# Two graph layers on one core: attention scores as additions of spread keys instead of a TensorE product, and the plain fp32 neighbour sum

## The chip, the cores and the metric

One core of a Trainium2 chip. The metric is the device time of one execution in microseconds (us). A core has five engines, each working through its own queue in order: TensorE (PE; its weight loads are shown as PEld), VectorE (DVE), ScalarE (ACT), GpSimd (POOL) and SyncE (SP, which issues transfers). They meet only through semaphores.

## The reference

128 graphs of 128 nodes, 256 features each, go through two layers; everything is fp32.

```
h  = relu(layernorm(x));  x = x + adj @ (h @ w0) + b0
h  = relu(layernorm(x))
proj = h @ fc_w + fc_b                      # 8 heads of 256
q, k = proj @ q_w + q_b, proj @ k_w + k_b   # one number per node and head
s  = leaky_relu(q + k^T + (1 - adj) * -1e9)
out = softmax(s) @ proj                     # per head
x  = x + sigmoid(concat_heads(out) @ fp_w + fp_b + h)
```

A score is the sum of one number of the row's node (the query) and one of the column's node (the key), plus a mask.

## The kernel before, in words

The graphs go in 64 pairs (`J` = 2). Per pair p, layer 0 first sums the neighbours (`aggregate`, lines 317 to 329), then multiplies with w0 (`transform`, 331), adds x and the bias (`residual0`, 537), takes the statistics (`stats1`, `mean1`) and turns the normalised tile (`transpose_h`, 339). Layer 1 works on heads whose fc and fp weights were multiplied together once in the setup (`fold`, lines 259 to 272): `project(p, q, n)`, n = 0 to 7, writes two heads of one graph into one PSUM bank; `attend(p, j, c)` multiplies them with the transposed attention rows of graph j and head group c (four heads), accumulating in `ybank`.

Precision comes from splitting: a matrix is stored as a high part rounded to fp32r and the rest (`_hi`, `_lo`), and `split` (246 to 251) sums three fp32r products of the parts. ACT writes the high part from PSUM (`g_high`, `pT_high`, `hT_high`), DVE the low part (`g_low`, `pT_low`, `hT_low`).

The scores are a TensorE product. `queries_keys` (349) makes 64 rows of keys and queries; DVE splits them (`kq_high`, `kq_parts`) and multiplies the keys with a mask of heads into `rk`, 32 partitions by 1024 (`spread`, 571); ACT writes the queries into the stationary tile `lq` (`queries`, 753). `scores(p, q, j, c)` (366) is one matmul with 512 columns into the only bank `sbank`; it waits until DVE has read the bank's last tenant. DVE adds the mask and takes the minimum (signs are turned) in `mask_min` (594), once per head, then `leaky` (605, a scalar_tensor_tensor of `att` with itself), ACT `exp` with row sums, DVE `inverse`, POOL `normalise` (918), PE `transpose_p`.

`aggregate` before: ACT writes the high part of h0 and of adjT (`h0_high`, `aT_high`), POOL the low parts (`h0_low`, `aT_low`), four times a 256-column and a 128-column fp32r matmul give two sums, ACT copies the small one (`ah_small`), DVE forms a difference (`ah_rest`) and POOL adds them (`ah_low`).

PSUM has eight banks: two for `front` (sums, kq, out0, h1T), `ybank`, `sbank`, and four `gbank`, which a ring of twelve tenants per pair shares, eight of `project` and four of `transpose_p` (`RING`, line 29; `ring_free`, 303).

Each engine's order within a pair is written out by hand in its `step(i, q)`. `pipeline` (172) runs steps before and after a hardware loop whose body holds two steps. PE at step i works on pair i, on the end of pair i - 1 and on layer 0 of pair i + 1. SP per pair loads `g_in` (x, adj, adjT: 512 KB) and stores `res` (256 KB). The setup begins with ten plain fp32 matmuls on ones (`warm`, 253), whose result nothing reads; the profile shows each plain fp32 matmul as two records.

```
def scores(p, q, j, c):
    bank = scores_free(NC * j + c, p)
    pe.matmul(bank[:], lq[q][j][:], rk[q][:, c * HC:(c + 1) * HC, :], start=True, stop=True)
```

Of the kernel before, what the change touches and what calls it, by code (L numbers as in the profile page):

```python
# [10 lines left out]
P = 128  # L11
D = 256
DT = D // P
H = 8
# [9 lines left out]
ROWS = 64  # L24
KEYS = 32
# [5 lines left out]
SRING = ((0, 0), (1, 0), (2, 0), (3, 0))  # L31
G_RANK = (0, 1, 0, 1, 0, 1, 1, 0)


def gnn_pair(nc, graph, identity, head_mask, row_coef, w0, bias0, fc_wT, fc_b, qk_w, q_b, k_b, fp_w, fp_b, out):
# [6 lines left out]
    with ExitStack() as ctx:  # L42
# [9 lines left out]
        def two(name, shape, dt=F32):  # L52
            return [sb(f"{name}{k}", shape, dt) for k in range(2)]

        def sems(name, n):
# [4 lines left out]
        hmask = sb("hmask", [P, H, P])  # L60
        coef = sb("coef", [P, 10])
# [4 lines left out]
        u_none = sb("u_none", [P, J, DT, ROWS])  # L66
# [3 lines left out]
        kqb2 = sb("kqb2", [P, 2])  # L70
# [6 lines left out]
        gate = sb("gate", [P, 8])  # L77
# [3 lines left out]
        early = sb("early", [P, 4, J * D])  # L81
        h0_f, xb = [[early[:, 2 * n + k, :].rearrange("p (j d) -> p j d", j=J) for k in range(2)] for n in range(2)]
        h0_hi, h0_lo = two("h0_hi", [P, J, D], F32R), two("h0_lo", [P, J, D], F32R)
        aT = two("aT", [P, J, 2, P], F32R)
        aT_lo, aT_hi = [[t[:, :, k, :] for t in aT] for k in range(2)]
        t_pos = two("t_pos", [P, J, P])
        ah_s, ah_d = sb("ah_s", [P, J, DT, P]), sb("ah_d", [P, J, DT, P])
        ah_hi, ah_lo = two("ah_hi", [P, J, DT, P], F32R), two("ah_lo", [P, J, DT, P], F32R)
        late = sb("late", [P, 8, J * D])
        x1, h1, feats_c, res = [[late[:, 2 * n + k, :].rearrange("p (j d) -> p j d", j=J) for k in range(2)]  # L90
                                for n in range(4)]
# [8 lines left out]
        kq_h, kq_t = sb("kq_h", [ROWS, P], F32R), sb("kq_t", [ROWS, P], F32R)  # L100
        lq = [two(f"lq{k}", [P, P], F32R) for k in range(2)]
        rk = two("rk", [P, H, P], F32R)
# [10 lines left out]
        fcT_sb = [w.rearrange("p (t d) -> p t d", d=D)  # L113
                  for w in (att_all[:, 0:H * D], late[:, 4:8, :].rearrange("p a b -> p (a b)"))]
# [3 lines left out]
        front = psum("front", [P, 2 * BANK])  # L118
        ybank = psum("ybank", [P, BANK])
        sbank = [psum("sbank", [P, BANK])]  # L120
        gbank = [psum(f"gbank{k}", [P, BANK]) for k in range(4)]
        sums = front[:].rearrange("p (j t c n) -> p j t c n", j=J, t=DT, c=2)
        kq = front[:, 0:BANK]
        out0 = kq.rearrange("p (j d) -> p j d", j=J)
        h1T = front[:, BANK:2 * BANK].rearrange("p (j t n) -> p j t n", j=J, t=DT)
# [3 lines left out]
        s_loaded, s_stored = sems("s_loaded", 2), sems("s_stored", 2)  # L129
# [4 lines left out]
        a_none, a_w0hi, v_w0lo, a_uhi, v_ulo, a_rk, v_lq = [  # L134
            sem(n) for n in ("a_none", "a_w0hi", "v_w0lo", "a_uhi", "v_ulo", "a_rk", "v_lq")]

        v_st0, v_mv0, g_ve0, g_rs0, g_nm0, g_nmr0 = [sem(n) for n in ("v_st0", "v_mv0", "g_ve0", "g_rs0", "g_nm0", "g_nmr0")]
        a_h0f, a_h0hi, g_h0lo, a_aThi, g_aTlo = [sem(n) for n in ("a_h0f", "a_h0hi", "g_h0lo", "a_aThi", "g_aTlo")]
        g_xb, g_t = sem("g_xb"), sem("g_t")
        pe_ah, a_ahhi, a_ahs, v_ah = [sem(n) for n in ("pe_ah", "a_ahhi", "a_ahs", "v_ah")]  # L140
        g_ahlo, pe_out0, v_x1 = [sem(n) for n in ("g_ahlo", "pe_out0", "v_x1")]
        v_st1, v_mv1, g_ve1, g_rs1, g_nm1, g_nmr1 = [sem(n) for n in ("v_st1", "v_mv1", "g_ve1", "g_rs1", "g_nm1", "g_nmr1")]
        a_h1, g_feats, pe_zT, a_hThi, v_hTlo = [sem(n) for n in ("a_h1", "g_feats", "pe_zT", "a_hThi", "v_hTlo")]
        pe_kq, v_kqh, v_kqt, v_rk, a_lq = [sem(n) for n in ("pe_kq", "v_kqh", "v_kqt", "v_rk", "a_lq")]
        pe_g, a_g, v_g = sems("pe_g", J * GC), sems("a_g", J * GC), sems("v_g", J * NC)
        pe_s, v_mx, v_leaky = sems("pe_s", J * NC), sems("v_mx", J * NC), sems("v_leaky", J * NC)
# [18 lines left out]
        def rows_of(u, j, dt):  # L165
            return u[:, j, dt, :].rearrange("p (k g c h) -> p k g c h", k=2, g=J, c=2)[:, :, j, :, :]

        def u_of(m, dt):
            return m[:, dt, :, D:D + 2].rearrange("p h k -> p k h").unsqueeze(2).bitcast(F32)\
                .broadcast_to([P, 2, 2, H])  # L170

        def pipeline(eng, step, behind, ahead):

            first = behind + 2
            last = first + (NP - ahead - first) // 2 * 2
            for i in range(-ahead, first):
                step(i, i % 2)
            with eng.Fori(first, last, 2) as i:
                step(i, first % 2)
                step(i + 1, 1 - first % 2)  # L180
            for i in range(last, NP + behind):
                step(i, i % 2)
# [15 lines left out]
        def _(sp):  # L198
# [5 lines left out]
            def setup():  # L204
                load(0, 0)
                weights(0)
                sp.dma_start(qk[:], qk_w).then_inc(s_small, 16)
                sp.dma_start(fcb[:], fc_b).then_inc(s_small, 16)
# [5 lines left out]
                sp.dma_start(coef[:], row_coef).then_inc(s_rest, 16)  # L214
                sp.dma_start(kqb2[:, 0:1], k_b.partition_broadcast(P)).then_inc(s_rest, 16)
                sp.dma_start(kqb2[:, 1:2], q_b.partition_broadcast(P)).then_inc(s_rest, 16)
# [12 lines left out]
            def store(p, q):  # L229
                sp.wait_ge(g_res, p + 1)  # L230
                sp.dma_start(out[p].rearrange("n (j d) -> n j d", j=J), res[q]).then_inc(s_stored[q], 16)
# [798 lines left out]
```

## Time and profile before

| | |
|---|---|
| time of the runs, median (3 runs, 1526.04 to 1527.67 us) | 1526.6 us |
| the profiled execution: its own time, its span | 1527.26 us, 1525.4 us |
| PE busy | 1510.1 us (99%) |
| PEld, DVE, ACT, POOL busy | 1339.6, 1343.5, 1205.1, 933.4 us (88%, 88%, 79%, 61%) |
| mean of the transfers | 37 GB/s, 55.89 MB |
| mean granted TensorE clock | 0.997 |

The span runs from the first to the last instruction. Busy time is the union of an engine's instructions, and these overlap: a matmul's record is longer than the distance to the next one, so costs on PE are read from starts, not from durations. An instruction's duration includes time in which it was held up.

### The profile page before, as it was taken

The numbers are of one execution on the slowest core, as the hardware profiler recorded it, in microseconds if no ns is written. First come the engines' busy times: TensorE is split into PE (matmuls) and PEld (weight loads), VectorE is DVE, ScalarE is ACT, GpSimd is POOL, SyncE is SP. The second block draws the span as 40 slices with busy tenths as digits, with TensorE's granted clock in tenths as the row PEclk, the third lists the DMA queues.
The fourth block names the chain that finished last, engine by engine and source line by source line (L and its number), as shares of the span: only waits on it lengthen the run. The fifth ranks groups of instructions, "written<-read, shape, count | busy, mean of one in ns | idle before, by whom it ended". The sixth has DMA issues, their size and how long they took to land.

```text
span 1525.4 us, 32795 instructions
## 1 busy us (share of the span) xinstructions
PE 1510.1 (99%) x9816; PEld 1339.6 (88%) x9816; DVE 1343.5 (88%) x4720; ACT 1205.1 (79%) x3674; POOL 933.4 (61%) x1226
## 2 busy tenths in 40 slices
PE   7999999999999999999999999999999999999998
PEld 6888888888888888888888888888888888888887
DVE  6988988988988989889889889889898898898886
ACT  5887878878878778878788787788788787887875
POOL 3656666566566566666665665665666666656653
PEclk9999999999999999999999999999999999999999
DMA  5101101101001011011011010010110110110100
GB/s 182 36 22 42 41 21 41 41 21 41 30 32 41 21 41 41 21 41 41 21 41 41 21 41 29 33 41 21 41 41 21 41 41 21 41 41 21 41 14 15
DMA packets 22579, 55.89 MB, mean 37 GB/s; under 512 B 2976, under 2 KB 5408, under 8 KB 22560
## 3 DMA queue, kind: packets, MB, share of 16 engines
q1 hardware_dynamic: 22560, 55.67, 10.6%
q8 instruction: 8, 0.13, 0.0%
q14 instruction: 11, 0.09, 0.0%
HBM read 38.88 MB, written 16.78 MB: 36 GB/s over the span
## 4 chain that ended last, share of the span: by engine, by line
PE 97%; DVE 1%; issue 1%; DMA 0%; ACT 0%; POOL 0%; SPq 0%; POOLq 0%; DVEq 0%
PE gbank L250 47%; PE ybank L250 23%; PE front L250 9%; PE gbank L375 7%; PE sbank L368 4%; PE front L327 3%; PE front L343 2%; PE gbank L270 1%; PE front L328 1%; DMA fcb<-fc_b_dram 0%; DVE att L601 0%; DVE att L608 0%; DVE g_lo L581 0%; DVE rk L573 0%; POOL att L921 0%
## 5 line engine op out<-in xcount | busy, mean ns | idle before, releaser
L921 POOL TENSOR_TENSOR att<-att,rinv 128x512 f32<-128x512 f32 x256 | 266.4, 1041 | 348.8 <-DVE rinv L613 348.8
L769 ACT ACTIVATE att<-att 128x128 f32<-128x128 f32 x1024 | 397.3, 393 | 65.8 <-DVE att L608 65.7
L250 PE MATMUL gbank<-m_hi,hT_lo 128*128 128x512 f32 x1024 | 417.4, 408 | 0.4 <-DVE g_lo L581 0.4
L250 PE MATMUL gbank<-m_lo,hT_hi 128*128 128x512 f32 x1024 | 405.2, 396 | 0.0
L250 PE MATMUL gbank<-m_hi,hT_hi 128*128 128x512 f32 x1024 | 404.1, 395 | 0.0
L762 ACT ACTIVATE g_hi<-gbank 128x512 fp32r<-128x512 f32 x512 | 286.8, 585 | 97.4 <-PE gbank L250 97.3
L581 DVE TENSOR_TENSOR g_lo<-gbank,g_hi 128x512 fp32r<-128x512 f32 x512 | 348.3, 680 | 15.4 <-ACT g_hi L762 15.4
L250 PE MATMUL ybank<-g_hi,pT_lo 128*128 128x256 f32 x1024 | 299.8, 293 | 0.0
L250 PE MATMUL ybank<-g_hi,pT_hi 128*128 128x256 f32 x1024 | 289.7, 283 | 0.0
L250 PE MATMUL ybank<-g_lo,pT_hi 128*128 128x256 f32 x1024 | 289.6, 283 | 0.0
L601 DVE CUSTOM_DVE_ANT_0 att<-sbank,t_pos 128x128 f32<-128x128 f32 x1024 | 236.3, 287 | 14.4 <-issue 14.4
L250 PEld LDWEIGHTS gbank<-m_hi,hT_hi 128*128 128x128 f32 x1024 | 194.6, 190 | 47.4
L608 DVE SCALAR_TENSOR_TENSOR att<-att 128x516 f32<-128x516 f32 x256 | 232.3, 927 | 0.0
L250 PEld LDWEIGHTS gbank<-m_hi,hT_lo 128*128 128x128 f32 x1024 | 194.3, 190 | 31.5 <-DVE g_lo L581 0.8
L250 PEld LDWEIGHTS gbank<-m_lo,hT_hi 128*128 128x128 f32 x1024 | 194.6, 190 | 29.7
L250 PEld LDWEIGHTS ybank<-g_lo,pT_hi 128*128 128x128 f32 x1024 | 195.9, 191 | 5.4
L250 PEld LDWEIGHTS ybank<-g_hi,pT_lo 128*128 128x128 f32 x1024 | 195.9, 191 | 0.2 <-DVE pT_lo L588 0.2
L769 ACT ACTIVATION_READ_ACCUMULATOR att<-att 128x1 f32 x1024 | 196.0, 191 | 0.0
L250 PEld LDWEIGHTS ybank<-g_hi,pT_hi 128*128 128x128 f32 x1024 | 195.8, 191 | 0.0
L588 DVE TENSOR_TENSOR pT_lo<-gbank,pT_hi 128x512 fp32r<-128x512 f32 x256 | 171.8, 671 | 1.0 <-ACT pT_hi L776 1.0
L898 POOL TENSOR_TENSOR h_lo<-early,h_hi 128x512 fp32r<-128x512 f32 x64 | 83.0, 1297 | 139.0 <-ACT h_hi L727 138.9
L375 PE MATMUL gbank<-ident,att 128*128 128x128 f32 x1024 | 153.4, 272 | 0.0
(101 smaller groups left out, 3042.3 us busy)
## 6 DMA issues: line engine op xcount, KB each, us to landing
g_in<-graph_dram SPq DMA_DIRECT2D x64, 512.0 KB, 3.3
out_dram<-late SPq DMA_DIRECT2D x64, 256.0 KB, 2.0
fp_sb<-fp_w_dram SPq DMA_DIRECT2D x4, 512.0 KB, 8.2
att<-fc_wT_dram SPq DMA_DIRECT2D x2, 512.0 KB, 6.4
late<-fc_wT_dram SPq DMA_DIRECT2D x2, 512.0 KB, 8.0
hmask<-head_mask_dram SPq DMA_DIRECT2D x1, 512.0 KB, 8.7
w_f<-w_dram SPq DMA_DIRECT2D x1, 256.0 KB, 7.2
b_row<-bias_dram SPq DMA_DIRECT2D x1, 128.0 KB, 6.9
```

What stands on the lines that cost most here:

```text
L250: mm = pe.matmul(out_ap, w, m, start=first and n == 0, stop=last and n == len(terms) - 1)
L327: pe.matmul(sums[:, j, dt, :, :], h0_hi[q][:, j, s], aT[q][:, j, :, :], start=True, stop=False)
L368: pe.matmul(bank[:], lq[q][j][:], rk[q][:, c * HC:(c + 1) * HC, :], start=True, stop=True)\
L375: mm = pe.transpose(bank[:, h * P:(h + 1) * P], att[j][c][:, h * P:(h + 1) * P], ident[:])
L581: dve.tensor_tensor(g_lo[j][:, s], bank[:], g_hi[j][:, s].bitcast(F32), ALU.subtract)\
L588: dve.tensor_tensor(pT_lo[j][:, hs, :], rows, pT_hi[j][:, hs, :].bitcast(F32), ALU.subtract)\
L601: r = dve.tensor_tensor_reduce(a[:, s], bank[:, s], t_pos[q][:, j, :], 1.0, 3.0e38, ALU.add, ALU.min, a[:, CH + h:CH + h + 1])
L608: dve.scalar_tensor_tensor(out=a, in0=a, scalar=SLOPE, in1=a, op0=ALU.mult, op1=ALU.min)\
L762: act.activation(g_hi[j][:, s], gbank[tenant(RING, 4, ("g", n), p)[0]][:], ACT.Copy).then_inc(a_g[n], 1)
L769: e = act.activation(a[:, s], a[:, s], ACT.Exp, scale=-1.0, bias=a[:, CH + h:CH + h + 1], accum_out=esum[j][c][:, h:h + 1])
L898: gp.tensor_tensor(h0_lo[q][:], h0_f[q], h0_hi[q][:].bitcast(F32), ALU.subtract)\
L921: gp.tensor_tensor(a, a, rinv[j][c][:].unsqueeze(2).broadcast_to([P, HC, P]), ALU.mult)\
```

## The change

- Scores: ACT adds the biases while it copies the key and query rows to SBUF (`kq_rows`). SP writes the 16 key rows to device memory (`keys_out`, 8 KB) and reads them back spread to all 128 partitions (`keys_in`, 8 KB per partition, 1 MB written to SBUF per pair). PE turns the rows once (`turn_queries`, one transpose), so that the queries lie one per partition and head, and ACT copies them (`queries`). POOL adds keys and mask for four heads at a time (`mask_keys`, four per pair, 128x512); DVE adds the query as a per-partition scalar and takes the minimum (`mask_min`, still once per head, now a tensor_scalar with an accumulator output on SBUF). The matmul `scores`, `kq_high`, `kq_parts`, `spread`, `rk`, `lq`, the head mask and its transfer are gone.
- `aggregate`: four plain fp32 matmuls of 128 columns on `h0_f` and adjT as loaded. `h0_high`, `aT_high`, `h0_low`, `aT_low`, `ah_small`, `ah_low` are gone; `ah_rest` now writes the low part itself.
- PSUM: `bank0` (sums, out0), `bank1` (h1T, kq, kqT), `ybank`, `tbank` for all `transpose_p`, and four `gbank` for the eight `project` alone.
- Orders of all engines are new. The loop body holds four steps (`U` = 4), layer 0 runs up to three pairs ahead on PE, `x1` and `feats` have four buffers. `load` runs six pairs ahead and stands in SP's queue before `keys_in`.
- Setup: 18 instead of 10 matmuls on ones; two small loads go to ACT's queue.

```diff
-RING = ((("t", 3), -1), (("g", 2), 0), (("g", 0), 0), (("g", 1), 0), (("g", 4), 0), (("t", 0), 0),
-        (("g", 5), 0), (("g", 3), 0), (("g", 7), 0), (("t", 1), 0), (("g", 6), 0), (("t", 2), 0))
+RING = ((3, 0), (6, 0), (7, 0), (4, 0), (1, 1), (0, 1), (2, 1), (5, 1))
+TRING = ((0, 0), (1, 0), (2, 0), (3, 0))
...
             def load(p, q):
                 if has(p - 2):
                     sp.wait_ge(a_h0f, 2 * (p - 1))
+                    sp.wait_ge(pe_ah, p - 1)
                     sp.wait_ge(g_xb, p - 1)
                     sp.wait_ge(g_t, p - 1)
-                    sp.wait_ge(g_aTlo, p - 1)
...
+            def keys_out(p, q):
+                sp.wait_ge(a_kq, p + 1)
+                sp.dma_start(key_rows[q], kq_sb[q][0:KEYS]).then_inc(s_rows[q], 16)
+            def keys_in(p, q):
+                sp.wait_ge(a_qs, p + 1)
+                sp.wait_ge(s_rows[q], 8 * (p - q % 2) + 16)
+                sp.dma_start(keys[q].rearrange("p j h n -> p (j h n)"),
+                             key_rows[q].rearrange("r n -> (r n)").partition_broadcast(P)).then_inc(s_keys[q], 16)
...
+                if has(i):
+                    store(i, q)
+                if later(i + 6):
+                    load(i + 6, (q + 2) % U)
+                if has(i + 3):
+                    keys_in(i + 3, (q + 3) % U)
+                if has(i + 4):
+                    keys_out(i + 4, q)
...
             def aggregate(p, q):
-                pe.wait_ge(g_h0lo, p + 1)
-                pe.wait_ge(g_aTlo, p + 1)
+                pe.wait_ge(a_h0f, 2 * (p + 1))
                 if has(p - 1):
-                    pe.wait_ge(v_kqt, p)
-                    pe.wait_ge(v_hTlo, p)
-
+                    pe.wait_ge(v_x1, p)
                 for j in range(J):
                     for dt in range(DT):
-                        s = slice(dt * P, (dt + 1) * P)
-                        pe.matmul(sums[:, j, dt, :, :], h0_hi[q][:, j, s], aT[q][:, j, :, :], start=True, stop=False)
-                        mm = pe.matmul(sums[:, j, dt, 1, :], h0_lo[q][:, j, s], aT_hi[q][:, j, :], start=False, stop=True)
+                        mm = pe.matmul(sums[:, j, dt, :], h0_f[q][:, j, dt * P:(dt + 1) * P], adjT_of(q)[:, j, :],
+                                       start=True, stop=True)
...
+            def turn_queries(p, q):
+                pe.wait_ge(a_kq, p + 1)
+                pe.transpose(kqT, kq_sb[q][:], ident[:]).then_inc(pe_kqT, 1)
...
             def transpose_p(p, j, c):
                 pe.wait_ge(g_norm[NC * j + c], p + 1)
-                bank = ring_free(("t", NC * j + c), p)
+                m, pair = tenant(TRING, 1, NC * j + c, p)[1:]
+                if has(pair):
+                    pe.wait_ge(v_pT[m], pair + 1)
...
             def mask_min(p, q, j, c):
-                dve.wait_ge(pe_s[NC * j + c], p + 1)
-                dve.memset(gate[:, 4 + NC * j + c:5 + NC * j + c], 0.0)
+                a = att[j][c]
+                dve.wait_ge(g_keys[NC * j + c], p + 1)
+                dve.wait_ge(a_qs, p + 1)
                 for h in range(HC):
                     s = slice(h * P, (h + 1) * P)
-                    r = dve.tensor_tensor_reduce(a[:, s], bank[:, s], t_pos[q][:, j, :], 1.0, 3.0e38,
-                                                 ALU.add, ALU.min, a[:, CH + h:CH + h + 1])
+                    r = dve.tensor_scalar(a[:, s], a[:, s], qs[q][:, j, c * HC + h:c * HC + h + 1], None, ALU.add,
+                                          ALU.min, accum_out=a[:, CH + h:CH + h + 1])
...
+            def kq_rows(p, q):
+                act.wait_ge(pe_kq, p + 1)
+                if has(p - 2):
+                    act.wait_ge(pe_kqT, p - 1)
+                    act.wait_ge(s_keys[q], 8 * (p - q % 2))
+                act.activation(kq_sb[q][0:ROWS], kq, ACT.Identity, bias=kq_bias[0:ROWS, 0:1]).then_inc(a_kq, 1)
...
+            def mask_keys(p, q, j, c):
+                gp.wait_ge(s_keys[q], 8 * (p - q % 2) + 16)
+                gp.wait_ge(g_t, p + 1)
+                if has(p - 1):
+                    gp.wait_ge(pe_pT[NC * j + c], p)
+                a = att[j][c][:, 0:CH].rearrange("p (h n) -> p h n", h=HC)
+                gp.tensor_tensor(a, keys[q][:, j, c * HC:(c + 1) * HC, :],
+                                 t_pos[q][:, j, :].unsqueeze(1).broadcast_to([P, HC, P]), ALU.add)\
+                  .then_inc(g_keys[NC * j + c], 1)
```

PE's new step, in order: turn_queries(i+1), project(i, 3), attend(i-1, 1, 1), transpose_p(i, 0, 0), project(i, 6), project(i, 7), aggregate(i+3), transpose_p(i, 0, 1), project(i, 4), attend(i, 0, 0), transpose_p(i, 1, 0), project(i+1, 1), transpose_h(i+2), attend(i, 0, 1), project(i+1, 0), queries_keys(i+2), transpose_p(i, 1, 1), attend(i, 1, 0), project(i+1, 2), project(i+1, 5), transform(i+3).

POOL's: mask_keys(i, 1, 0), mask_keys(i, 1, 1), residual1(i-2), normalise(i, 0, 0), inputs(i+2), normalise(i, 0, 1), feats(i), normalise(i, 1, 0), the small ones of variance1(i+2) and variance0(i+4), normalise(i, 1, 1), mask_keys(i+1, 0, 0), mask_keys(i+1, 0, 1).

## Rows read from the trace of the kernel before

**Rows 1.** The page: busy time by engine, and the chain that ended last.
```profile
PE 1510.1 (99%) x9816; PEld 1339.6 (88%) x9816; DVE 1343.5 (88%) x4720; ACT 1205.1 (79%) x3674; POOL 933.4 (61%) x1226
...
PE 97%; DVE 1%; issue 1%; DMA 0%; ACT 0%; POOL 0%; SPq 0%; POOLq 0%; DVEq 0%
```

**Rows 2.** Stretches: us, busy PE, PEld, DVE, ACT, POOL, then clock, DMA share, GB/s.
```profile
0.00:20.00 20.00, 14.67 (x60) 12.62 (x61) 8.87 (x22) 7.99 (x17) 8.08 (x19) 0.83 0.94 312
20.00:40.00 20.00, 16.91 (x93) 13.67 (x91) 18.97 (x68) 12.22 (x30) 8.63 (x13) 1.00 0.14 48
...
700.00:900.00 200.00, 200.00 (x1319) 178.08 (x1318) 177.95 (x630) 159.85 (x484) 124.92 (x164) 1.00 0.09 31
```

**Rows 3.** Timeline of PE, one pair of the loop: start us, us, instruction.
```profile
805.23 0.28 PE L327 MATMUL front<-aT,h_hi 128*128 128x256 f32 x1
...
806.10 0.45 PE L368 MATMUL sbank<-rk,lq 128*128 128x512 f32 x1
806.38 0.28 PE L250 MATMUL ybank<-g_hi,pT_lo 128*128 128x256 f32 x1
...
809.20 0.41 PE L368 MATMUL sbank<-rk,lq 128*128 128x512 f32 x1
809.44 0.60 PE L375 MATMUL gbank<-ident,att 128*128 128x128 f32 x4
809.80 0.48 PE L250 MATMUL gbank<-m_hi,hT_lo 128*128 128x512 f32 x1
...
828.44 0.28 PE L327 MATMUL front<-aT,h_hi 128*128 128x256 f32 x1
```

**Rows 4.** Timeline of PE in the setup, plain fp32, narrow stretches.
```profile
4.70 0.39 PE L257 MATMUL gbank<-ones 128*128 128x128 f32 x2
...
4.92 0.28 PE L257 MATMUL gbank<-ones 128*128 128x128 f32 x1
```

**Rows 5.** Groups of DVE: shapes and count | busy us, mean ns | idle before.
```profile
L601 DVE CUSTOM_DVE_ANT_0 att<-sbank,t_pos 128x128 f32<-128x128 f32 x1024 | 236.3, 287 | 14.4 <-issue 14.4
L608 DVE SCALAR_TENSOR_TENSOR att<-att 128x516 f32<-128x516 f32 x256 | 232.3, 927 | 0.0
...
L573 DVE TENSOR_TENSOR rk<-hmask,kq_t 32x1024 fp32r<-32x1024 f32 x64 | 78.8, 1232 | 2.2
...
L563 DVE TENSOR_SCALAR kq_h<-front,kq_bias,coef 64x128 fp32r<-64x128 f32 x64 | 26.0, 406 | 4.9
L568 DVE SCALAR_TENSOR_TENSOR kq_t<-front,kq_bias,kq_h 64x128 fp32r<-64x128 f32 x64 | 19.7, 308 | 0.1
```

**Rows 6.** Groups of POOL.
```profile
L921 POOL TENSOR_TENSOR att<-att,rinv 128x512 f32<-128x512 f32 x256 | 266.4, 1041 | 348.8 <-DVE rinv L613 348.8
L907 POOL TENSOR_TENSOR ah_lo<-ah_d,ah_s 128x512 fp32r<-128x512 f32 x64 | 83.1, 1299 | 19.3 <-DVE ah_d L534 19.3
L914 POOL TENSOR_TENSOR early<-g_in,b_row 128x512 f32<-128x512 f32 x64 | 83.1, 1299 | 0.0
...
L898 POOL TENSOR_TENSOR h_lo<-early,h_hi 128x512 fp32r<-128x512 f32 x64 | 83.0, 1297 | 139.0 <-ACT h_hi L727 138.9
...
L903 POOL TENSOR_TENSOR aT<-g_in,aT 128x256 fp32r<-128x256 f32 x64 | 47.4, 740 | 6.1 <-ACT aT L731 6.1
```

**Rows 7.** Timelines of DVE and POOL where both work on SBUF.
```profile
810.50 2.37 DVE L608 SCALAR_TENSOR_TENSOR att<-att 128x516 f32<-128x516 f32 x2
...
810.41 1.30 POOL L937 TENSOR_TENSOR late<-sg,late 128x512 f32<-128x512 f32 x1 [0.80 <-ACT sg L788]
...
34.56 2.29 DVE L573 TENSOR_TENSOR rk<-hmask,kq_t 32x1024 fp32r<-32x1024 f32 x1
...
35.85 1.93 POOL L916 TENSOR_SCALAR t_pos<-g_in 128x256 f32<-128x256 f32 x1
```

**Rows 8.** Transfers: count, KB each, median us from issue to landing.
```profile
g_in<-graph_dram SPq DMA_DIRECT2D x64, 512.0 KB, 3.3
out_dram<-late SPq DMA_DIRECT2D x64, 256.0 KB, 2.0
```

More of the change, by code:

```diff
@@ L255, in warm @@
                 pe.wait_ge(g_ones, 1)
-                for n in range(10):
-                    pe.matmul(gbank[3][:, 0:P], ones[:], ones[:], start=True, stop=True)
+                for n in range(18):
+                    pe.matmul(tbank[:, 0:P], ones[:], ones[:], start=True, stop=True)
             def fold(n):
@@ L622, in step @@
             def step(i, q):
+                if later(i + 1):
+                    hT_low(i + 1, (q + 1) % U)
+                if has(i):
+                    g_low(i, 1)
+                    mask_min(i, q, 0, 0)
+                    leaky(i, 0, 0)
+                    mask_min(i, q, 0, 1)
                 if has(i - 1):
@@ L637, in step @@
+                    g_low(i, 0)
+                    mask_min(i, q, 1, 1)
+                    g_low(i, 5)
+                    g_low(i, 2)
+                    leaky(i, 1, 1)
+                    inverse(i, 0, 1)
                 if has(i - 1):
-                    add_feats(i - 1, 1 - q)
+                    add_feats(i - 1, (q + 3) % U)
+                if later(i + 2):
+                    residual0(i + 2, (q + 2) % U)
                 if has(i):
-                    g_low(i, 1)
-                    mask_min(i, q, 1, 1)
@@ L662, in step @@
-                if later(i + 1):
-                    hT_low(i + 1, 1 - q)
+                if later(i + 4):
+                    mean0(i + 4, q)
                 if has(i):
                     g_low(i, 6)
+                    g_low(i, 4)
+                    g_low(i, 7)
                     pT_low(i, 1, 0)
-                if has(i + 1):
-                    kq_high(i + 1)
                 if later(i + 3):
-                    mean0(i + 3, 1 - q)
-                if has(i + 1):
-                    kq_parts(i + 1)
-                    spread(i + 1, 1 - q)
+                    ah_rest(i + 3, (q + 3) % U)
@@ L831, in _ @@
+                if has(i + 1):
+                    exp(i + 1, 0, 0)
             setup()
-            pipeline(act, step, 1, 2)
+            pipeline(act, step, 1, 4)
         @block.gpsimd
@@ L849, in setup @@
                 shift0(0, 0)
-                aT_low(0, 0)
-                h0_low(0, 0)
                 gp.wait_ge(s_layer0, 48)
                 inputs(0, 0)
-                ah_low(0, 0)
                 variance1(0, 0)
@@ L958, in step @@
-                if later(i + 1):
-                    shift0(i + 1, 1 - q)
-                if has(i - 1):
-                    feats(i - 1, 1 - q)
-                if later(i + 1):
-                    inputs(i + 1, 1 - q)
-                    h0_low(i + 1, 1 - q)
-                if later(i + 2):
-                    aT_low(i + 2, q)
-                    variance0(i + 2, q)
+                    residual1(i - 2, (q + 2) % U)
                 if has(i):
                     normalise(i, 0, 0)
+                if later(i + 2):
+                    inputs(i + 2, (q + 2) % U)
@@ L971, in _ @@
+                if has(i):
+                    normalise(i, 1, 1)
+                if has(i + 1):
+                    mask_keys(i + 1, (q + 1) % U, 0, 0)
+                    mask_keys(i + 1, (q + 1) % U, 0, 1)
+                if later(i + 4):
+                    shift0(i + 4, q)
             setup()
-            pipeline(gp, step, 2, 2)
+            pipeline(gp, step, 2, 4)
 def kernel(x, adj, L0_gnn_weight, L0_gnn_bias, L1_gnn_fc_w, L1_gnn_fc_b, L1_gnn_q_w, L1_gnn_q_b,
```

481 lines of the change are left out of this document (193 added, 288 removed).

## Prediction

> **What bounds the kernel now.** First the page: PE is busy 99% of the span and the chain that ended last is PE for 97% [rows 1]. A busy PE can still be stretched by waits, so the stretches come next: from 700 to 900 us PE is busy 200.00 of 200.00 us at clock 1.00, with DVE at 177.95, ACT at 159.85 and POOL at 124.92 [rows 2]. Then the timeline: the first matmul of `aggregate` stands at 805.23 and again at 828.44, one pair later [rows 3], and in between each start follows the last by the matmul's own pace. So a pair costs 23.21 us of pure PE work, and 64 pairs 1485 us of the 1525.4. The remaining 40 are setup, filling and end. What shortens PE's list shortens the run, as long as the other engines deliver.
>
> **PE's list, part by part.** Costs are distances between starts.
> - Score matmuls, four per pair, removed. One before `attend` costs 806.38 - 806.10 = 0.28 us, one before transposes 809.44 - 809.20 = 0.24 [rows 3]; two of the four stand like either. Together -1.04 us.
> - `aggregate` in fp32. Now 806.10 - 805.23 = 0.87 us [rows 3]. A plain fp32 matmul is two records; in the setup, once the pace rises, two records of 128 columns take 4.92 - 4.70 = 0.22 us, each with its weight load [rows 4]. Four matmuls are 0.88 us: +0.01. Plain fp32 gives PE nothing here; it only relieves ACT and POOL.
> - `turn_queries`, one transpose. Four cost 809.80 - 809.44 = 0.36 us [rows 3], so one lies between 0.09 (a quarter) and 0.36 (all of it being entry and exit). It stands alone between other matmuls, which makes me take 0.20.
> - `queries_keys`, `project`, `attend`, `transform` and the other transposes keep their counts; only neighbours change.
>
> Sum -0.83 us: 22.38 per pair, and 64 x 0.83 = 53 us. With the transpose at its two ends it is 60 or 43.
>
> **The ends of the run.** In the setup two small loads come earlier and eight more matmuls on ones keep PE at work; the mean clock of the first 20 us is 0.83 with PE busy 14.67 [rows 2], so the most there is to win is about 3 us of clock and some of the 5.3 idle; I take -2. Against it the keys of pair 0 now need a store and a spread load before its first score: 2.0 us for 256 KB [rows 8] for the store, about 5 for the 1 MB (next part). PE has `project` and layer 0 of pairs 1 and 2 to do meanwhile, but in the prologue these are chains of their own through DVE, POOL and ACT. PE idled 3.1 us from 20 to 40 [rows 2]; I add 5 there and 3 for the last pair, whose step has no work of a next pair. Together +6, between 0 and +14.
>
> **What has to stay hidden.**
> - DVE: 177.95 of 200 is 20.65 us per pair [rows 2]. Gone are `spread`, `kq_high`, `kq_parts`: (78.8 + 26.0 + 19.7) / 64 = 1.95 us [rows 5]. `mask_min` is priced as now, 16 x 287 ns recorded [rows 5]; it reads SBUF in place of PSUM and could be down to half of that or some tenths of a us dearer. About 18.7 of 22.38 us, 84%: less than today's 89%.
> - ACT loses four passes per pair and two small ones, and gets two small ones: under today's 80%.
> - POOL: 124.92 of 200 is 14.5 us per pair [rows 2]. Gone are `ah_low`, `h0_low`, `aT_low`: (83.1 + 83.0 + 47.4) / 64 = 3.34. New are four `mask_keys` of 128x512: between 1.04 us (`normalise`, one operand short) and 1.30 (`inputs`, whose second operand is repeated along the outer axis just as here) [rows 6]; the form decides, 1.30. That gives 14.5 - 3.3 + 5.2 = 16.4 us, 73%. Cost on the end: nothing, with 6 us of slack per pair as cover; without it every us above 22.38 costs 64 us.
> - SP's queue: `load`(i+6) waits for the mask of pair i+4, which POOL makes after two `mask_keys`, `residual1` and one `normalise`: 2.6 + 1.3 + 1.0 + 2.4 = 7.3 us into its step. Behind it stands `keys_in`(i+3), behind that `keys_out` and the next pair's `store`. 256 KB more cost 3.3 - 2.0 = 1.3 us [rows 8], so load and keys together (1.5 MB) land 3.3 + 4 x 1.3 = 8.5 us later, at about 16. POOL wants them near the end of its step, 2 x 1.3 before 22.38, at 19.8. Margin some 4 us. `keys_out` waits for ACT at its step's start, a pair before it is read back.
> - `tbank`: a transpose block waits for `pT_low` of the one before. The shortest gap, with `project`(4) and `attend` between, is about 2.8 us of PE, against two passes of 0.6 to 0.7 us: enough if ACT and DVE are not more than 1 us late.
> - The doubled loop body: the stretch of the loop shows PE without a gap [rows 2], so there is no branch to save, and I count 0.
>
> **A rule against it.** DVE and POOL keep each other out: two `leaky` from 810.50 take 2.37 us while POOL's add on SBUF runs from 810.41 for 1.30, and `rk` takes 2.29 at 34.56 while POOL's next instruction is stretched to 1.93 [rows 7]. The mean of `leaky` is 927 ns [rows 5], so now one in four is held for about a us. The SBUF page of the Trainium skill (section Who interferes with whom) says that a DVE instruction with two SBUF inputs and a GpSimd instruction that reads SBUF exclude each other for a whole instruction; by that, the trace agrees. The same section counts tensor_scalar among the holders, but not the form that writes out its accumulator, which `mask_min` is; no row here shows that form on SBUF. If `leaky` is held each time, DVE grows by 3 x 1.1 = 3.3 us to 22.0, just under PE.
>
> **Sum.** 1525.4 - 53 + 6 = 1478.4 us of span; what lies around it is 1527.26 - 1525.4 = 1.9. So 1480 us, against 1527.26 of the profiled execution, which is 0.7 above the median of the runs.
>
> **Rivals.**
> - *Small stalls.* All four `leaky` held: DVE at 22.0 of 22.38 leaves PE waiting for `g_low` or `pT_low` now and then. At 0.3 to 0.5 us per pair +19 to +32: 1500 to 1512. For it: POOL's list grows and its order is new. Against: DVE sheds 2 us first. Chance 0.20.
> - *Dear fp32.* fp32 records of 128 columns at twice 0.11 us, if their weight loads do not hide behind real operands: `aggregate` grows by 0.88 per pair, and 1480 + 56 = 1536. The setup's pace [rows 4] speaks against it. Chance 0.03, slower.
> - *Level.* Stalls of about 0.7 us per pair eat the gain: 1480 + 45 = 1525. Chance 0.03.
> - *DVE shut out.* If the 16 `mask_min` of a pair are holders too, each of 20 instructions meets a POOL busy for 73% of the time and waits on average half of 1.2 us: 20 x 0.73 x 0.6 = 8.8 us. DVE needs 27.5 per pair and becomes the bound: 64 x 27.5 + 40 = 1800. It decides as soon as DVE's waits pass 23.21 - 18.7 = 4.5 us per pair; at half that rate the kernel is no slower. For it: the mechanism is there [rows 7]. Against: it has one SBUF input, like `g_low`, which no row shows held. Chance 0.05, slower.
>   By the exception in the page's section (the Trainium skill, SBUF, Who interferes with whom) it would not happen.
> - *Keys late.* Landing later than 19.8 in POOL's step shifts the whole pair; each us past the margin of 4 costs 64 us. 12 us in place of 8.5 would still do, 14 would give 23.9 per pair or some 1575. Nothing in the loop is that slow (3.3 us for 512 KB [rows 8]). Chance 0.05, slower.
> - *Another order fault* of the same size, mostly a late `pT_low` behind the single `tbank`: 0.03, slower.
>
> **How the numbers follow.** The forecast, PE still without gaps, has 0.61; its own range is 1470 to 1492, from the transpose's two ends and the ends of the run. Small stalls carry 0.20 up to 1512. A measurement of this kernel tells 0.2% (3 us) from no change. Faster 0.81 (0.61 + 0.20), same 0.03, slower 0.16. The range 1468 to 1514 leaves out the slower cases and a little below.
>
> **What would show it.** Right: in mid-run PE busy 200 of 200, `aggregate`'s first matmul every 22.4 us, its eight records 0.88 us apart in all; `mask_keys` 1.30 us each and POOL near 73%; `mask_min` 0.2 to 0.3 us and never stretched by POOL, `leaky` with a mean above 927 ns; key loads landing within 8 us and POOL never waiting for them in the loop. Wrong: PE idle in the loop with DVE's `att`, `pT_lo` or a key transfer named as releaser; a period near or above 23.2; `mask_min` at a us or more.

## The result: 1509.1 us, faster by 1.2% where 3.1% was forecast

| | before | after |
|---|---|---|
| median of the runs | 1526.57 us (1526.04 to 1527.67, 4 runs) | 1509.07 us (1508.52 to 1509.40, 4 runs) |
| ratio, 95% interval | | 0.9884 (0.9872 to 0.9896) |
| profiled execution, span | 1527.26, 1525.4 | 1508.82, 1507.0 |
| mean granted clock of TensorE | 0.997 | 0.987 |
| forecast | | 1480 (1468 to 1514) |

The sign is right and the time lies within the range, but the gain is 17.5 us where 46.6 were forecast. The page of the kernel after, in the lines that answer to [rows 1], with q14, a queue that carries instructions, DVE's among them (packets, MB, share):

```profile
span 1507.0 us, 32030 instructions
...
PE 1463.6 (97%) x9640; PEld 1309.5 (87%) x9640; DVE 1249.0 (83%) x4267; ACT 1078.9 (72%) x3480; POOL 1079.1 (72%) x1292
...
q14 instruction: 83, 0.68, 0.2%
...
PE 88%; issue 5%; ACT 3%; DVE 2%; POOL 1%; DMA 0%; DVEq 0%; POOLq 0%; SPq 0%; ACTq 0%
```

PE is no longer full (97% of the span, 99% before), and 5% of the chain is "issue", time in which an engine waited for nothing that the profile shows. Where it lies is seen in stretches (columns: us, busy time of PE, PEld, DVE, ACT and POOL with their instructions, granted clock, DMA share, GB/s):

```profile
0.00:20.00 20.00, 18.30 (x98) 16.21 (x99) 10.14 (x31) 6.92 (x16) 4.95 (x18) 1.00 0.90 314
20.00:40.00 20.00, 12.15 (x65) 10.47 (x63) 10.56 (x38) 7.56 (x20) 5.99 (x14) 0.74 0.06 16
700.00:900.00 200.00, 193.20 (x1286) 172.95 (x1285) 165.14 (x564) 143.33 (x458) 143.93 (x171) 0.99 0.19 74
245.70:249.30 3.60, 1.45 (x12) 1.06 (x11) 1.81 (x7) 0.00 (x0) 0.00 (x0) 0.85 0.02 5
249.30:262.70 13.40, 13.40 (x79) 12.11 (x78) 11.86 (x45) 10.63 (x42) 9.27 (x8) 0.91 0.30 110
```

In mid-run PE is busy 193.20 of 200 us, where [rows 2] had 200.00. The loss is not spread evenly. The first matmul of `aggregate` marks each pair, as in [rows 3]; here are three in a row of PE's timeline:

```profile
236.65 1.05 PE L323 MATMUL bank<-g_in,h_f 128*128 128x128 f32 x8
...
262.78 1.05 PE L323 MATMUL bank<-g_in,h_f 128*128 128x128 f32 x8
...
285.02 1.05 PE L323 MATMUL bank<-g_in,h_f 128*128 128x128 f32 x8
```

The second distance is 22.24 us, and so are nearly all of the others. The first is 26.13. Twelve distances are long, each four pairs after the last: six of 26.1 to 26.3 us and six of 24.5 to 24.8. That is once per turn of the loop, whose body now holds four steps. Above 22.24 they are 6 x 4.0 + 6 x 2.35 = 38 us. What happens in one of them, on DVE's timeline:

```profile
242.83 0.68 DVE L517 TENSOR_TENSOR ah_lo<-bank,ah_hi 128x512 fp32r<-128x512 f32 x1
247.49 0.69 DVE L539 TENSOR_TENSOR hT_lo<-bank,hT_hi 128x512 fp32r<-128x512 f32 x1 [3.98 <-issue]
```

`ah_rest` is the last instruction of DVE's loop body and `hT_low` the first. Between them DVE stands for 3.98 us, and nothing it waits for is late. PE feels it, because `queries_keys` needs `hT_lo`:

```profile
248.24 0.32 PE L256 MATMUL bank<-hT_hi,u_lo 128*32 128x128 f32 x1 [2.15 <-DVE hT_lo L539]
```

The lists of waits of DVE and of PE count them (us in total, times, longest):

```profile
DVE hT_lo L539 <- issue: 48.6, 12, 4.2
...
PE bank L256 <- DVE hT_lo L539: 26.6, 12, 2.4
```

The stretches above show the second part of the price: after the pause the granted clock is 0.85 to 249.3 and 0.91 from there to 262.7 us, which is 3.6 x 0.15 / 0.5 + 13.4 x 0.09 / 0.5 = 3.5 us at the lower of the two levels, 1.2 GHz in place of 2.4. In the next pause, from 337.4 to 354 us, it stays at 1.00. So it goes by turns, and that is why six distances are about 24.6 and six 26.2. PE's 26.6 us of waits and six times the difference of 1.6 us make 36 of the 38. So the sum of the forecast lacks one item: 1525.4, less 0.97 for each of the 64 pairs (62 us), plus 38 for the pauses, plus about 5 at the ends, is 1506, where 1507.0 was measured.

The other engines, in the list of groups:

```profile
L856 POOL TENSOR_TENSOR att<-keys,t_pos 128x512 f32<-128x512 f32 x256 | 328.6, 1294 | 150.4 <-PE tbank L370 149.7 <-DMA keys<-key_rows 0.7
L563 DVE TENSOR_SCALAR_CACHE_REDUCE att<-att,qs 128x128 f32<-128x128 f32 x1024 | 291.1, 340 | 0.0
L570 DVE SCALAR_TENSOR_TENSOR att<-att 128x516 f32<-128x516 f32 x256 | 189.4, 740 | 2.2
L563 DVE DVE_READ_ACCUMULATOR att<-att,qs 128x1 f32 x1024 | 83.8, 82 | 0.0
```

```profile
keys<-key_rows SPq DMA_DIRECT2D x64, 1024.0 KB, 5.3
g_in<-graph_dram SPq DMA_DIRECT2D x64, 512.0 KB, 3.3
```

`mask_keys` takes the 1.29 us that was forecast, the keys land after 5.3 us, and POOL waited for them 0.7 us in the whole run.

### The profile page after: what moved, and what is told of

Read it like the earlier page. It is cut to its first block, busy times and chain, and to the rows that moved or that the text cites. A ratio compares the mean times of both kernels' runs of the same rounds, so it can differ in the third digit from the quotient of the medians.

```text
span 1507.0 us, 32030 instructions
## 1 busy us (share of the span) xinstructions
PE 1463.6 (97%) x9640; PEld 1309.5 (87%) x9640; DVE 1249.0 (83%) x4267; ACT 1078.9 (72%) x3480; POOL 1079.1 (72%) x1292
## 4 chain that ended last, share of the span: by engine, by line
PE 88%; issue 5%; ACT 3%; DVE 2%; POOL 1%; DMA 0%; DVEq 0%; POOLq 0%; SPq 0%; ACTq 0%
PE gbank L256 43%; PE ybank L256 22%; PE bank L256 9%; PE tbank L370 7%; PE bank L323 4%; PE bank L341 1%; ACT g_hi L707 1%; PE gbank L276 1%; ACT pT_hi L721 1%; ACT h L683 1%; DVE ah_lo L517 1%; DVE hT_lo L539 1%; PE bank L355 0%; DMA fp_sb<-fp_w_dram 0%; ACT ah_hi L678 0%
## 5 line engine op out<-in xcount | busy, mean ns | idle before, releaser
L856 POOL TENSOR_TENSOR att<-keys,t_pos 128x512 f32<-128x512 f32 x256 | 328.6, 1294 | 150.4 <-PE tbank L370 149.7
L256 PE MATMUL gbank<-m_hi,hT_lo 128*128 128x512 f32 x1024 | 427.9, 418 | 0.0
L863 POOL TENSOR_TENSOR att<-att,rinv 128x512 f32<-128x512 f32 x256 | 289.5, 1131 | 143.9 <-DVE rinv L575 142.1
L721 ACT ACTIVATE pT_hi<-tbank 128x512 fp32r<-128x512 f32 x256 | 153.4, 599 | 285.5 <-PE tbank L370 285.5
L546 DVE TENSOR_TENSOR g_lo<-gbank,g_hi 128x512 fp32r<-128x512 f32 x512 | 336.6, 678 | 24.6 <-ACT g_hi L707 22.2
L563 DVE TENSOR_SCALAR_CACHE_REDUCE att<-att,qs 128x128 f32<-128x128 f32 x1024 | 291.1, 340 | 0.0
L553 DVE TENSOR_TENSOR pT_lo<-tbank,pT_hi 128x512 fp32r<-128x512 f32 x256 | 176.4, 689 | 92.9 <-ACT pT_hi L721 85.0
L570 DVE SCALAR_TENSOR_TENSOR att<-att 128x516 f32<-128x516 f32 x256 | 189.4, 740 | 2.2
```

Source lines behind the costliest of these rows:

```text
L256: mm = pe.matmul(out_ap, w, m, start=first and n == 0, stop=last and n == len(terms) - 1)
L546: dve.tensor_tensor(g_lo[j][:, s], bank[:], g_hi[j][:, s].bitcast(F32), ALU.subtract)\
L553: dve.tensor_tensor(pT_lo[j][:, hs, :], rows, pT_hi[j][:, hs, :].bitcast(F32), ALU.subtract)\
L563: r = dve.tensor_scalar(a[:, s], a[:, s], qs[q][:, j, c * HC + h:c * HC + h + 1], None, ALU.add, ALU.min, accum_out=a[:, CH + h:CH + h + 1])
L570: dve.scalar_tensor_tensor(out=a, in0=a, scalar=SLOPE, in1=a, op0=ALU.mult, op1=ALU.min)\
L721: act.activation(pT_hi[j][:, c * HC:(c + 1) * HC, :], rows, ACT.Copy).then_inc(a_pT[NC * j + c], 1)
```

## The experiments

**Theory A**: DVE's loop body of four steps is too long to stay where the engine holds its instructions (304 instructions in the trace, with waits, register work and accumulator reads; the body of two steps before had 165), so each backward branch makes it fetch them again, and DVE stands for some 4 us. What speaks for it before any experiment: queue q14, which carries instructions, moved 50 packets of 8 KB between 400 and 1300 us after the change (the first line below) and none in that stretch before (where the view lists q1 alone, the second line). **Theory B**: the pause is a wait of the new order (`hT_lo`, the keys, the port that DVE and POOL share) that falls due every fourth pair, and the branch has nothing to do with it.

```profile
q14 instruction: 50, 0.41, 0.2%
```

```profile
q1 hardware_dynamic: 10944, 29.89, 9.6%
```

### The loop written out, on all engines and on DVE alone

```diff
-            with eng.Fori(first, last - U + 1, U) as i:
-                for k in range(U):
-                    step(i + k, (first + k) % U)
+            for i in range(first, last):
+                step(i, i % U)
```

> The changed kernel with its hardware loop written out: every engine runs all 64 pairs as straight code, nothing else differs. Theory A (the loss sits at the loop's backward branch, where VectorE stands for some 4 us with nothing to wait for, 12 times): the 12 long intervals between the aggregates (six of 26.1 to 26.3 us, six of 24.5 to 24.75) go back to 22.24 us, which is 6 x 4.0 + 6 x 2.35 = 38 us, so about 1471 us. Theory B (the stalls come from the new order: a wait on hT_lo, the keys or the port that falls due every fourth pair): the time stays at 1509 us and the long intervals stay where they are.

> The changed kernel with the loop written out on VectorE alone; the other four engines keep their loop of four steps. Theory A with VectorE as the only engine whose loop body is too long to stay in its instruction buffer: about 1471 us, as with all engines written out. If TensorE's or ScalarE's branch costs too: between 1471 and 1509 us. Theory B: 1509 us.

All engines: 1470.26 us, ratio 0.9626 (0.9613 to 0.9639). DVE alone: 1469.82 us, 0.9627 (0.9614 to 0.9640). The page and the mid-run stretch of the second:

```profile
span 1468.0 us, 31821 instructions
...
PE 1450.4 (99%) x9640; PEld 1299.4 (89%) x9640; DVE 1247.2 (85%) x4267; ACT 1078.8 (73%) x3480; POOL 1077.3 (73%) x1292
...
q14 instruction: 49, 0.40, 0.1%
```

```profile
700.00:900.00 200.00, 200.00 (x1343) 179.62 (x1341) 173.18 (x595) 150.14 (x487) 151.09 (x181) 1.00 0.22 83
```

PE is full again, every distance from the fourth on is 22.23 or 22.24 us (in every version of the new kernel the first three belong to the filling of the pipeline), and the line "hT_lo <- issue" is gone from the list of waits. The pauses cost 1509.07 - 1469.82 = 39.3 us, all of it on DVE's branch: with DVE's loop gone, those of PE, ACT, POOL and SP cost nothing measurable. Straight code is fetched too (49 packets), but DVE waited for none of it. Theory B has fallen. This version is also faster than both kernels.

### Half as many branches

```diff
-            last = first + (NP - ahead - first) // U * U
+            last = first + (NP - ahead - first) // 8 * 8
...
-            with eng.Fori(first, last - U + 1, U) as i:
-                for k in range(U):
+            with eng.Fori(first, last - 7, 8) as i:
+                for k in range(8):
                     step(i + k, (first + k) % U)
```

> The changed kernel with eight steps in the loop body in place of four, on all engines: 6 backward branches in place of 12. Theory A: half of the 38 us goes, so about 1490 us, and the long intervals stand 8 pairs apart. Theory B (a stall every fourth pair): 1509 us, intervals as they are.

1507.74 us, 0.9865 (0.9850 to 0.9880): the long distances do stand 8 pairs apart and number six, but they are 24.98, 28.04, 28.97, 29.59, 29.71 and 31.69 us. A branch now costs (sum less 6 x 22.24) / 6 = 6.6 us in place of 3.2. The lists of waits of DVE, PE, PE's weight loads and ACT, and the queues, say why:

```profile
DVE hT_lo L539 <- issue: 21.1, 5, 4.3
...
PEld ybank L256 <- issue: 12.2, 6, 2.5
PE gbank L256 <- issue: 10.4, 6, 2.2
...
ACT kq_sb L695 <- issue: 4.8, 4, 1.3
```

```profile
q8 instruction: 92, 1.51, 0.4%
q14 instruction: 99, 0.81, 0.2%
```

With eight steps PE's body and ACT's are too long as well: q8, which moved 15 packets before, moved 92, and PE has pauses of its own of up to 2.5 us. (That q8 serves PE is an inference: with every engine's loop written out it moved 78 packets of 16 KB, with DVE's alone 15, and of the other four engines PE runs by far the most instructions.) The number of branches alone isn't the price; what each has to fetch, on how many engines, is the other factor. My expectation of half the cost took it as fixed.

### The kernel before, with a body of four steps

```diff
-            with eng.Fori(first, last, 2) as i:
-                step(i, first % 2)
-                step(i + 1, 1 - first % 2)
+            with eng.Fori(first, last - 3, 4) as i:
+                for k in range(4):
+                    step(i + k, (first + k) % 2)
```

> The kernel before with four steps in its loop body in place of two, nothing else. VectorE's body grows from 165 to 330 instructions, more than the changed kernel's. Theory A: its some 14 branches each hold VectorE for about 4 us, of which 2.1 to 4 reach TensorE: 1526.6 + 14 x 3.1 = about 1570 us (1556 to 1583), with fresh instruction transfers inside the loop. Theory B: 1526.6 us, as before.

1569.40 us, 1.0276 (1.0261 to 1.0290), as theory A had it. None of the rest of the change is in this kernel. Its body on DVE is 322 instructions in the trace, where the expectation counted 330. One of its queues and the waits of DVE and PE, from the profiled execution:

```profile
q14 instruction: 83, 0.68, 0.2%
```

```profile
DVE att L601 <- issue: 33.6, 77, 1.4
...
DVE pT_lo L588 <- issue: 23.2, 13, 2.0
...
PE sbank L368 <- DVE att L601: 33.3, 15, 2.7
```

`pT_low` is the first instruction of this kernel's body on DVE; its 13 waits for nothing are new. So is a second stop of up to 1.4 us a few instructions later, in `mask_min` (L601; before, its longest wait for nothing was 0.3 us). PE feels both through the scores. Thirteen distances between aggregates are long, most of them 25.9 us against 23.2; in sum that is 37 us, and the profiled execution took 1563.18 us, the shortest of the five (clock 0.996, the others 0.992 to 0.994). By the medians, unrolling by four alone costs this kernel 42 us, about what the changed kernel paid at its branches.

### The kernel before, DVE written out (control)

The edit is that of the first experiment, for DVE alone.

> Control: the kernel before with VectorE's loop written out, nothing else. Its body of two steps showed no idle time at the branch and no instruction transfer inside the loop, so nothing is to be had: 1526.6 us, within 2. If writing the loop out brings something of its own (no register arithmetic, no branch at all), it is faster than 1523 us, and part of what the changed kernel gained by it was not the stall.

1527.43 us, 1.0005 (0.9996 to 1.0014): no gain. A body of two steps (165 instructions) costs nothing at its branch, and what the changed kernel gained by writing the loop out was the pause and nothing else.

### A shorter body, the loop kept

```diff
-                for h in range(HC):
-                    s = slice(h * P, (h + 1) * P)
-                    r = dve.tensor_scalar(a[:, s], a[:, s], qs[q][:, j, c * HC + h:c * HC + h + 1], None, ALU.add,
-                                          ALU.min, accum_out=a[:, CH + h:CH + h + 1])
-                r.then_inc(v_mx[NC * j + c], 1)
+                rows = a[:, 0:CH].rearrange("p (h n) -> p h n", h=HC)
+                dve.tensor_tensor(rows, rows, qs[q][:, j, c * HC:(c + 1) * HC].unsqueeze(2).broadcast_to([P, HC, P]),
+                                  ALU.add).then_inc(v_sum[NC * j + c], 1)
+                dve.wait_ge(v_sum[NC * j + c], p + 1)
+                dve.tensor_reduce(a[:, CH:CH + HC], rows, mybir.AxisListType.X, ALU.min).then_inc(v_mx[NC * j + c], 1)
```

> The changed kernel with its loop of four steps kept on every engine, but fewer instructions in VectorE's body: mask_min adds the query column to a whole tile with one tensor_tensor (the column broadcast over 128 elements) and takes the four minima with one tensor_reduce, in place of four tensor_scalar with accumulation and the four accumulator reads behind them. VectorE's body goes from 240 instructions and 64 accumulator reads (304) to 208. The results are the same. If the length of the body is what makes each branch cost, the idle time of VectorE at hT_lo after each branch is gone and the time is about 1470 us, as with the loop written out. If a branch costs that much whatever the body's length, it stays at about 1509 us. If VectorE gets too dear (the two long instructions may take more than the 1.07 us of the four short ones, and the addition can wait for the port that GpSimd uses), the steady interval rises over 22.24 us, 0.1 us of it being 6 us of the time.

1510.16 us (1504.47 to 1521.02), 0.9899 (0.9872 to 0.9925): the time says nothing, the profile does. DVE has no "issue" line left, and q14 moved nothing between 400 and 1300 us (20 packets in the whole run). But:

```profile
PE 1472.3 (98%) x9640; PEld 1294.6 (86%) x9640; DVE 1410.6 (94%) x2731; ACT 1087.9 (72%) x3480; POOL 1147.5 (76%) x1292
...
q14 instruction: 20, 0.16, 0.0%
```

```profile
L563 DVE TENSOR_TENSOR att<-att,qs 128x512 f32<-128x512 f32 x256 | 307.2, 1200 | 0.0
...
L566 DVE TENSOR_REDUCE att<-att 128x4 f32<-128x512 f32 x256 | 175.7, 686 | 8.8
```

The tile costs DVE about 1.9 us in place of 1.07. The reduction takes 686 ns, but the addition takes 1200 in the mean: over its 256 instructions half last 0.93 us or less and a quarter 1.79 or more. It has two inputs in SBUF, like `leaky`. That POOL holds it up is read from the trace: the 72 additions of less than 0.70 us have 0.08 us of POOL's instructions beside them in the mean, the 115 longest (1.3 us and more) 1.34. `mask_min` as the change writes it never was held: 327 to 352 ns, with 0.25 us of POOL beside it in the mean. One bound went and another came, of the same size by chance. To part them, the same edit with DVE's loop written out:

> The short mask_min (one tensor_tensor and one tensor_reduce a tile) with VectorE's loop written out. The run with the short mask_min in the loop gave 1510 us without any idle time of VectorE at the branch, but with VectorE busy 94% of the span and intervals of up to 23.7 us between aggregates. If that time is VectorE's dearer work alone and a branch with 208 instructions is free, writing the loop out changes nothing: 1510 us, within 4. If the branch still costs in a way the trace does not show, about 1470 to 1480 us.

1511.75 us (1507.22 to 1527.84), 0.9889 (0.9874 to 0.9904). Writing the loop out changes nothing here beyond the spread of the runs, which is wide for the short form (1504 to 1521 and 1507 to 1528 us). So the loss of the short form is DVE's dearer work. That a branch over 208 instructions costs nothing rests on the profile more than on the time: no pause and no packet.

### How short is short enough

The same edit for some tiles only: the last of a pair's four (280 instructions), or the last two (256).

```diff
+                if NC * j + c >= J * NC - 1:
...
+                    return
                 for h in range(HC):
```

> The changed kernel, loop kept, with the short mask_min for one of the four tiles of a pair (the last): VectorE's body is 280 instructions with its accumulator reads, in place of 304. Between 208, which showed no stall, and 304, which did. If a body of 280 is still too long: the idle time of some 4 us at each of 12 branches stays, and about 1510 us. If it fits: about 1472 us (VectorE is some 0.8 us a pair dearer, which its idle time holds).

> The same with the short mask_min for two of the four tiles: VectorE's body is 256 instructions with its accumulator reads. If it fits: about 1472 to 1480 us, since VectorE's 1.6 us more a pair still fit in its idle time of about 3 us a pair, or nearly. If it is still too long: about 1512 us, with the 12 idle times of some 4 us.

280: 1471.00 us, 0.9632 (0.9619 to 0.9646). 256: 1471.21 us, 0.9638 (0.9625 to 0.9651). The page and the groups of the first:

```profile
PE 1451.7 (99%) x9640; PEld 1300.6 (88%) x9640; DVE 1268.8 (86%) x3883; ACT 1078.7 (73%) x3480; POOL 1103.5 (75%) x1292
...
q14 instruction: 22, 0.18, 0.0%
```

```profile
L572 DVE TENSOR_SCALAR_CACHE_REDUCE att<-att,qs 128x128 f32<-128x128 f32 x768 | 218.5, 340 | 0.0
...
L565 DVE TENSOR_TENSOR att<-att,qs 128x512 f32<-128x512 f32 x64 | 56.1, 876 | 0.0
```

This is the sharpest of the experiments. The loop is kept on every engine, DVE does more work than in the changed kernel (1268.8 us against 1249.0), and yet the time falls by 38 us, with 24 instructions of 304 gone from the body. q14 is silent in the loop. In these runs 280 stays and 304 is fetched again. But the edit moves two things at once: the short form also stands in the straight code ahead of the loop, so with one short tile a pair DVE's body begins 30 instructions earlier as well (after 415 in place of 445 in the trace), with two 60. Where exactly the edge lies, and how much of it is the body's length and how much its place, isn't shown.

### The terms of the sum

Three runs price the parts of PE's list, two of them on the kernel with DVE written out, where PE is full.

The turn twice:

```diff
+                pe.transpose(kqT, kq_sb[q][:], ident[:])
                 pe.transpose(kqT, kq_sb[q][:], ident[:]).then_inc(pe_kqT, 1)
```

> The changed kernel with VectorE's loop written out (1469.8 us) and every turn_queries transpose issued twice, into the same place. The prediction priced one at 0.20 us a pair (0.09 to 0.36): 1469.8 + 64 x 0.20 = 1482.6 us (1475.6 to 1492.8). If the pair lost 0.97 us because that term was too dear (1.04 saved, 0.07 paid): 64 x 0.07 = 4.5 us, so about 1474 us.

1476.56 us, 6.7 us more, 0.105 a pair. Neither value of mine: it lies between them, near the low end of the range.

Four more matmuls:

```diff
+                if n in (3, 6, 4, 1):
+                    pe.matmul(bank[:].rearrange("p (h d) -> p h d", h=2), hT_hi[q][:, j, 0, :], m_hi[:, 0, hs, 0:D],
+                              start=True, stop=True)
```

> The changed kernel with VectorE's loop written out (1469.8 us) and four more fp32r matmuls of 512 columns a pair, each with its own stationary tile, written into a bank just ahead of project, which overwrites it: as much TensorE work as the four scores matmuls that the change took away. By the prediction's term 4 x 0.26 = 1.04 us a pair: 1469.8 + 66.6 = 1536 us. If the removed scores matmuls were worth less than that (0.88 us a pair, what 64 pairs need to explain a smaller gain): 1526 us.

1527.98 us, 58.2 us more, 0.91 a pair, or 0.227 each. The prediction had 0.26.

`aggregate` in plain fp32 alone, in the kernel before (the removal of the high and low parts and of their waits is left out of the diff):

```diff
-                        pe.matmul(sums[:, j, dt, :, :], h0_hi[q][:, j, s], aT[q][:, j, :, :], start=True, stop=False)
-                        mm = pe.matmul(sums[:, j, dt, 1, :], h0_lo[q][:, j, s], aT_hi[q][:, j, :], start=False, stop=True)
+                        mm = pe.matmul(sums[:, j, dt, 1, :], h0_f[q][:, j, s], adjT_of(q)[:, j, :],
+                                       start=True, stop=True)
```

> The kernel before with one part of the change alone: aggregate as four plain fp32 matmuls of the unrounded h0 and adjacency, without the high and low parts of the two, so that ScalarE's h0_high, aT_high and ah_small and GpSimd's h0_low, aT_low and ah_low fall away and VectorE writes ah_lo itself. By the prediction's term (+0.01 us a pair on TensorE) nothing: 1526.6 us, within 3 us. If ScalarE's or GpSimd's freed time was worth something to TensorE: below 1523. If the plain fp32 matmuls are dearer in the loop than in the setup: 0.2 us a pair would be 1539.

1524.78 us, 0.9988 (0.9979 to 0.9997): 1.7 us less, 0.03 a pair. POOL fell to 96.24 busy us of 200 in mid-run from 124.92 [rows 2], and the time hardly moved: as forecast, the plain form relieves the other engines and gives PE next to nothing.

## Why the prediction was wrong, step by step

**The step that failed** is "The doubled loop body: the stretch of the loop shows PE without a gap [rows 2], so there is no branch to save, and I count 0." The step asked only what the branch of before could give back. It said nothing of what a longer body could cost, and it gave no range for it, though the trace of before couldn't show it: its body of two steps (165 instructions on DVE) stays in place, with no packet of q14 between 400 and 1300 us. What the runs showed in its place: 12 branches that each fetch instructions again, 39.3 us in all (1509.07 against 1469.82 with DVE's loop written out, 1471.00 with a body of 280 in place of 304). With that term the forecast of 1480 would have been 1519; without the pauses the kernel takes 1470, at the low end of my own range of 1470 to 1492. That 1509 lies inside the wider range of 1468 to 1514 is luck: the upper part of it was there for *Small stalls*, another mechanism.

The Trainium skill (Runtime: NRT & Kernel Launch, section Instruction fetch mechanics) says that a taken branch whose target is outside the pages held makes the engine fetch the target before it can go on. The runs agree (five packets a turn with a body of 304, none with one of 280), and that section had belonged beside the step. The Trainium skill gives 512 instructions for most engines there, in blocks of 256 of which two are held. Taken as a limit of 512 for the body, it would have missed this case, where 304 were already too many. By the Trainium skill's figures (an estimate) a body of over 257 that begins late in a block reaches into a third one, so the section need not contradict these runs; none of them tests it.

**The other steps.**
- *Period.* Forecast 22.38 us (-0.83), measured 22.24 (-0.97). The three experiments add up to -0.91 - 0.03 + 0.105 = -0.83, the forecast sum, by errors that cancel: a score-sized matmul is worth 0.227 and not 0.26, the turn 0.105 and not 0.20, `aggregate` -0.03 and not +0.01. The missing 0.14 lies in none of them. Another way to divide the same 0.97 is to sum over 30 pairs of mid-run from each matmul's start to the next start, before and with DVE written out. That gives 1.04 for the scores, just as forecast, +0.03 for the turn, +0.03 for `aggregate` (0.89 in place of 0.86), +0.17 for `project`, -0.08 for the transposes of `att` (1.50 to 1.42) and -0.08 for `queries_keys` (0.80 to 0.72). "only neighbours change" took the last three as zero, and `project` alone moved by 0.17. That the new neighbours are the reason is argued from this. The two ways divide the gain differently and no run isolates a neighbour, so only the total is firm. It made the kernel about 9 us faster than forecast.
- *Ends.* Forecast +6, measured 1468.0 - (1525.4 - 64 x 0.965) = +4.4, from the profile with DVE written out. The first 20 us did gain (PE busy 18.30, clock 1.00, against 14.67 and 0.83), the next 20 lost (12.15 against the 16.9 that [rows 2] shows).
- *DVE.* Forecast 18.7 us a pair, measured 173.18 / 200 x 22.24 = 19.3, 87%. `mask_min` is dearer: its records are 340 ns where I took 287, and from one start to the next it takes 0.27 us where it took 0.21 (the accumulator read of some 83 ns was there before too). That is 0.9 us a pair. `leaky` sheds 0.8, and the rest of the difference is `pT_low` (+0.3) and small rises of others.
- *POOL.* Forecast 16.4, measured 151.09 / 200 x 22.24 = 16.8; `mask_keys` 1294 ns as forecast.
- *Keys, `tbank`, SP's queue.* In the loop PE waits for `hT_lo` alone, never for `pT_low`, and POOL waited 0.7 us for keys in the whole run. POOL's 149.7 us of waiting for PE's transposes cost PE nothing. The margins held.
- *The lock of DVE and POOL.* The part on `mask_min` was right, though it is a little longer than the 0.2 to 0.3 us named: 327 to 352 ns, never stretched. The exception that the Trainium skill (SBUF — State Buffer, section Who interferes with whom) makes for the form with an accumulator held. The forecast that `leaky` would be held more often was wrong: its mean fell from 927 [rows 5] to 740 ns although POOL does more. In the trace 63 of its 256 instructions lasted over 1.3 us before, 7 after. Where in the step an instruction falls seems to count for more than how busy the other engine is; no run isolates this.

**The rivals.** The time fell into the range of *Small stalls* (1500 to 1512, chance 0.20), but not by its mechanism: PE waited for no `g_low` or `pT_low` in the loop, and the stalls are few and long. The rest of the rivals didn't occur: `aggregate` takes 0.89 us a pair, `mask_min` was never held, and the keys were there in time. What would have shown the forecast wrong was named as "PE idle in the loop with DVE's `att`, `pT_lo` or a key transfer named as releaser"; PE was idle with DVE's `hT_lo` named, and DVE's own wait had no releaser at all. That is the line to look for.

## What to carry to other kernels

Before a loop is unrolled further, count the instructions of its body on each engine, with waits, register work and accumulator reads, and keep a price for a branch that has to fetch: here 3.2 us per turn with a body of 304 on DVE and nothing with one of 280. In a profile it shows as an engine idle for several us at the first instruction of its body with "issue" as releaser, and as packets on an instruction queue inside the loop. The cure can be as small as one tile's worth of instructions merged, or the loop of that one engine written out; both gave 1470 to 1471 us, 3.7% under the kernel before.

## What the runs showed of the hardware that was not expected

- An instruction fetch comes in packets of 8 KB on q14 (0.68 MB in 83), and at the branch where DVE stands from 336.4 to 340.5 us three of them were moved at 336.1, 338.6 and 341.1 us (each within 0.25 us, read from the DMA row of 334 to 344). DVE went on before the third was moved. So the pause holds the distance between two small packets, 2.5 us, and not the time of their bytes; what fills the 1.9 us from the second packet to DVE's next start isn't shown.
- A turn fetches more than the body holds. With DVE's loop written out, q14 moved 23 packets between 400 and 1300 us, while DVE ran 72 instructions for each pair of 22.24 us, some 2900: about 127 instructions a packet (an estimate). In the changed kernel each of the ten turns in that stretch moved five packets, by the same estimate some 640 instructions for a body of 304.
- Straight code costs DVE nothing: 64 pairs written out, 49 packets, no "issue" wait in the loop. Only the jump back does.
- A pause of 2.2 us in PE's work isn't the whole price. In six of twelve cases the granted clock went to its lower level for about 3.5 us afterwards and added some 1.6 us; with the pauses gone the mean clock of the run rose from 0.987 to 0.995.
- On DVE, four additions that write out their minimum cost 1.07 us a tile and were never held by POOL; one long addition of two SBUF inputs and a reduction cost 1.9, for two instructions in place of eight (accumulator reads counted).
